# Attention phase of a three-phase kernel: the rate goes into the clip, one exponential serves two heads, and queries and keys are stacked by common instructions, with a copy on GpSimd

## The chip, the cores and the metric

The kernel runs on one core of one Trainium2 chip. A core has TensorE (matrix multiplications and transposes), VectorE, ScalarE, GpSimd and a DMA queue engine (SyncE), which run their own instruction streams and wait for one another by semaphores. The metric is the device time of one execution in microseconds, lower is better.

## The reference

A tower of four state-space layers makes `h` (2048 tokens in 8 sequences of 256, 256 features). The second phase, to which the change belongs, adds an attention whose scores are Gaussian kernels of the distance between query and key. With H = 16 heads of D = 16:

```python
qh = (q @ Wq).reshape(Bq, Sq, H, D).transpose(0, 2, 1, 3)      # likewise kh, vh
q_norm = jnp.sum(qh * qh, axis=-1, keepdims=True)              # likewise k_norm
qk = jnp.einsum('bhsd,bhtd->bhst', qh, kh)
dist = jnp.maximum(q_norm - 2.0 * qk + jnp.swapaxes(k_norm, -2, -1), 0.0)
scores = jnp.exp(-gamma[None, :, None, None] * SCALE * dist)
scores = jnp.where(mask, scores, 0.0)                          # mask: triu, k=1
out = jnp.einsum('bhst,bhtd->bhsd', scores, vh)
return out.transpose(0, 2, 1, 3).reshape(Bq, Sq, H * D) @ Wo
```

The input `q` is the layer norm of `h`. A third phase, two layers of windowed attention with a gated feed-forward part, follows.

## The kernel before, in words

`attention_phase` handles the 8 sequences (s = 0 to 7) one after the other, each as two tiles (t = 0, 1) of 128 tokens, in a software pipeline. Every engine has a function `half(h)` that lists, in a fixed order written by hand, what it does for the sequences that are in flight; TensorE's half h projects sequence h, turns sequence h - 1 and scores sequence h - 2. TensorE runs halves 2 to 10 in the block after the tower (the first sequence's part runs earlier, from `opening` in the tower's last steps and from `first`). GpSimd's and VectorE's half with number h + 3, and ScalarE's with number h + 4, hold the work that belongs to TensorE's half h. Below, "half 2" and so on are TensorE's numbers.

All matmuls are done in split precision: a value is rounded to float32r (the "hi" part) and the remainder ("lo") is kept beside it. For the distances the split is folded into the contraction: each head has a row of ROW = 64 columns per token in `qs` and `ks`. In `qs` it holds q hi, q hi again, q lo, the squared norm's hi and lo, two ones and zeros; in `ks` it holds -2k hi, -2k lo, -2k hi again, two ones, the norm's hi and lo and zeros. One matmul over these 64 rows then gives q_norm - 2 qk + k_norm. The steps for one tile:

- `project_qk` (TensorE) writes queries and keys, 512 columns, into one PSUM bank.
- `square` (ScalarE) and `norms` (VectorE) make the 32 squared norms.
- `query_hi` and `key_hi` (ScalarE, lines 1138, 1139, 1146, 1147) write the hi parts, each twice: four copies of 256 columns.
- `stack` (VectorE, lines 1309 to 1320) writes the lo parts and the norms: six instructions.
- `turn` (TensorE, line 925) transposes eight pairs of heads, queries or keys of one tile, into two banks. `turned_q` and `turned_k` (1024 columns each) copy the result to `qt` and `kt`. ScalarE does `turned_q` for both tiles and `turned_k` for tile 1, VectorE `turned_k` for tile 0 (line 1328).

Per sequence the heads go in eight pairs c: `distances(s, c, b)` (lines 938, 941) fills two banks with 384 columns per head, `clip` (VectorE, line 1336, 768 columns) takes the maximum with 0 into `dist`, `kernel_exp` (ScalarE, line 1178) makes one exponential of 384 columns per head with the scale operand `gsc[:, h:h + 1]`, `mask` (GpSimd, line 1476) clears the masked triangles, and `values(s, q, b)` (lines 957, 959) multiplies four heads by the values; the result goes through `output_hi`, `output_lo`, `project_out` and `add_output` into X. A clip needs the exponentials of two pairs earlier, since `dist` holds two pairs.

TensorE's order in half h, with b = h - 1 and c = h - 2, is: `project_v` of both tiles, `turn_x`, `distances(c, 2)`, `turn(b, 0, 0)`, `distances(c, 3)`, `turn(b, 0, 1)`, `turn(b, 1, 0)`, `distances(c, 4)`, `turn(b, 1, 1)`, `distances(c, 5)`, `values(c, 0)`, `distances(c, 6)`, `values(c, 1)`, `distances(c, 7)`, `project_out`, `distances(b, 0)`, `values(c, 2)`, `project_qk` of tile 0, `distances(b, 1)`, `values(c, 3)`, `project_qk` of tile 1. In `turn(b, t, i, bank)` i = 0 are the queries and i = 1 the keys. `values(c, 0)` writes the bank that `turn(b, 1, 0)` used and so waits for `qt_done`, `turned_q(b, 1)`.

GpSimd also does `scale_h` and `bias_h` (the tower's last norm, 512 columns each), `rstd`, and in its half h + 3 the order is: `bias_h`, `qkv_rest` (in four of the halves, a split of the third phase's weights), masks 2, 3 and 4, `scale_h`, masks 5 and 6, `rstd`, mask 7, mask 0 of the next sequence, `rstd`, mask 1. `scale_h` is there up to half 5 and `bias_h` up to half 6. Right after its first such list, between mask 1 and the `bias_h` that belongs to half 2, stands `masks()`, which fills constants of the third phase.

## Time and profile before

| | |
|---|---|
| median of 3 runs | 1275.93 us (1275.78 to 1276.22) |
| profiled execution, own time | 1278.31 us |
| its span, first to last instruction | 1276.4 us |
| mean granted TensorE clock | 0.983 of full speed |
| busy: TensorE / VectorE / ScalarE / GpSimd | 1209.8 / 984.7 / 860.2 / 621.2 us |
| turnings of the second phase | from 511.8 to 644.5 us of the span |
| exponentials of the second phase | from 526.6 to 661.7 us of the span |

The profile is of one execution. "Busy" of an engine is time in which one of its instructions ran, matmuls with their modelled ends. A time in brackets after an instruction is the idle time of its engine before it, with the instruction that ended it.

### The profile page before, as it was taken

The numbers are of one execution on the slowest core, as the hardware profiler recorded it, in microseconds if no ns is written. First come the engines' busy times: TensorE is split into PE (matmuls) and PEld (weight loads), VectorE is DVE, ScalarE is ACT, GpSimd is POOL, SyncE is SP. The second block draws the span as 40 slices with busy tenths as digits, with TensorE's granted clock in tenths as the row PEclk, the third lists the DMA queues.
The fourth block names the chain that finished last, engine by engine and source line by source line (L and its number), as shares of the span: only waits on it lengthen the run. The fifth ranks groups of instructions, "written<-read, shape, count | busy, mean of one in ns | idle before, by whom it ended". The sixth has DMA issues, their size and how long they took to land.

```text
span 1276.4 us, 26138 instructions
## 1 busy us (share of the span) xinstructions
PE 1209.8 (95%) x8899; PEld 1028.5 (81%) x8899; DVE 984.7 (77%) x2624; ACT 860.2 (67%) x1989; POOL 621.2 (49%) x678
## 2 busy tenths in 40 slices
PE   5999999999999999799978799999999999999998
PEld 3799988988888989577756567888888888888898
DVE  5767676666667777789878988888888888888754
ACT  2455766675556556689964668778777777777764
POOL 6523441361145243455434568556655567556543
PEclk9899999999999999899989999999999999999999
DMA  7400010001000000300110002000100000000001
GB/s 172 115 2 15 2 66 0 14 33 33 0 8 1 1 1 1 77 10 18 58 54 17 1 5 95 6 5 6 48 3 6 22 6 13 22 17 18 22 10 42
DMA packets 39615, 33.25 MB, mean 26 GB/s; under 512 B 16774, under 2 KB 36178, under 8 KB 39506
## 3 DMA queue, kind: packets, MB, share of 16 engines
q1 hardware_dynamic: 38610, 29.74, 7.7%
q0 software_dynamic: 768, 2.10, 1.0%
q8 instruction: 60, 0.98, 0.3%
q14 instruction: 49, 0.40, 0.1%
q10 hardware_dynamic: 128, 0.04, 0.0%
HBM read 25.84 MB, written 4.19 MB: 24 GB/s over the span
## 4 chain that ended last, share of the span: by engine, by line
PE 45%; DVE 6%; issue 3%; POOL 2%; ACT 2%; DVEq 0%; ACTq 0%; POOLq 0%
PE w_ps_p L1914 3%; PE w_ring L1975 3%; PE w_ring L1976 3%; PE w_ring L1873 3%; PE w_ring L1977 3%; PE w_ring L1875 3%; PE w_ring L1874 3%; PE w_ps_a L1932 2%; PE w_ring L1987 2%; PE a_ps L925 2%; PE w_ps_d L1907 2%; PE w_ps_d L1904 2%; PE w_ring L1891 2%; PE w_ring L1988 2%; PE w_ring L1991 1%
## 5 line engine op out<-in xcount | busy, mean ns | idle before, releaser
L392 ACT ACTIVATE t_gf<-t_ps_f,t_fb_cur 128x512 f32<-128x512 f32 x128 | 87.9, 687 | 159.8 <-PE t_ps_f L298 156.6
L542 DVE TENSOR_TENSOR t_g_lo<-t_gf,t_g_hi 128x512 fp32r<-128x512 f32 x128 | 93.3, 730 | 69.3 <-ACT t_g_hi L394 68.9
L311 PE MATMUL t_ps_o<-t_w_hi,t_g_hi 128*128 128x256 f32 x512 | 144.6, 282 | 0.1
L312 PE MATMUL t_ps_o<-t_w_lo,t_g_hi 128*128 128x256 f32 x512 | 143.0, 279 | 0.0
L313 PE MATMUL t_ps_o<-t_w_hi,t_g_lo 128*128 128x256 f32 x512 | 142.9, 279 | 0.0
L695 POOL TENSOR_TENSOR t_rs<-t_ve,t_neghalf 128x4 f32<-128x4 f32 x32 | 40.9, 1277 | 159.8 <-DVE t_ve L503 158.2
L296 PE MATMUL t_ps_f<-t_nh,t_w_hi 128*128 128x512 f32 x256 | 102.6, 401 | 1.5 <-DVE t_nl L518 0.8
L2988 POOL TENSOR_TENSOR w_m<-w_m 128x512 f32<-128x512 f32 x64 | 84.2, 1316 | 36.9 <-DVE w_m L2631 36.8
L298 PE MATMUL t_ps_f<-t_nl,t_w_hi 128*128 128x512 f32 x256 | 100.3, 392 | 0.0
L297 PE MATMUL t_ps_f<-t_nh,t_w_lo 128*128 128x512 f32 x256 | 100.0, 391 | 0.0
L311 PEld LDWEIGHTS t_ps_o<-t_w_hi,t_g_hi 128*128 128x128 f32 x512 | 96.2, 188 | 4.1 <-issue 0.9
L312 PEld LDWEIGHTS t_ps_o<-t_w_lo,t_g_hi 128*128 128x128 f32 x512 | 96.7, 189 | 2.5
L313 PEld LDWEIGHTS t_ps_o<-t_w_hi,t_g_lo 128*128 128x128 f32 x512 | 96.8, 189 | 0.0
L2674 DVE COPY w_pt<-w_ps_p 128x384 f32<-128x384 f32 x128 | 70.5, 551 | 31.4 <-PE w_ps_p L1914 29.9
L1975 PE MATMUL w_ring<-w_nh,w_w_hi 128*128 128x256 f32 x318 | 93.5, 294 | 0.0
L1976 PE MATMUL w_ring<-w_nh,w_w_lo 128*128 128x256 f32 x318 | 88.8, 279 | 0.0
L1977 PE MATMUL w_ring<-w_nl,w_w_hi 128*128 128x256 f32 x318 | 88.7, 279 | 0.0
L2999 POOL TENSOR_TENSOR w_pr<-w_pr,w_rinv 128x256 f32<-128x256 f32 x64 | 39.3, 614 | 101.0 <-DVE w_rinv L2668 101.0
L1873 PE MATMUL w_ring<-qkv_hi,w_ah 128*128 128x512 f32 x188 | 80.6, 429 | 6.7 <-DVE w_al L2613 5.7
L3004 POOL TENSOR_TENSOR w_h_lo<-w_gate,w_h_hi 128x256 fp32r<-128x256 f32 x75 | 54.6, 737 | 60.1 <-ACT w_h_hi L2413 60.1
L394 ACT ACTIVATE t_g_hi<-t_gf 128x512 fp32r<-128x512 f32 x128 | 80.9, 632 | 4.1
L1178 ACT ACTIVATE a_e<-a_dist,a_gsc 128x384 f32<-128x384 f32 x128 | 70.2, 621 | 8.3 <-DVE a_dist L1336 6.8
(369 smaller groups left out, 4285.0 us busy)
## 6 DMA issues: line engine op xcount, KB each, us to landing
t_raw<-in_L_tok_w SPq DMA_DIRECT2D x8, 1024.0 KB, 5.4
out<-X SPq DMA_DIRECT2D x14, 256.0 KB, 2.2
raw<-in_L_ffn_wqkv SPq DMA_DIRECT2D x2, 1536.0 KB, 6.9
raw<-in_L_ffn_w SPq DMA_DIRECT2D x4, 640.0 KB, 4.8
w_raw_o<-out SPq DMA_DIRECT2D x8, 256.0 KB, 2.8
w_xs<-X SPq DMA_DIRECT2D x14, 127.0 KB
w_raw<-in_L_ffn_w SPq DMA_DIRECT2D x2, 640.0 KB
t_raw_d<-in_L_tok_D SPq DMA_DIRECT2D x4, 256.0 KB
```

Source lines behind the costliest of these rows:

```text
L296: pe.matmul(ps_f[:, j % 2, :], w1_hi[:, c, col], nh[1][:, c, :], start=(c == 0), stop=False)
L297: pe.matmul(ps_f[:, j % 2, :], w1_lo[:, c, col], nh[1][:, c, :], start=False, stop=False)
L298: mm = pe.matmul(ps_f[:, j % 2, :], w1_hi[:, c, col], nl[1][:, c, :], start=False, stop=(c == DC - 1))
L311: pe.matmul(out, g_hi[:, j % 4, tok], w2_hi[:, j, :], start=(j == 0 and t % 2 == 0), stop=False, skip_group_check=True)
L312: pe.matmul(out, g_hi[:, j % 4, tok], w2_lo[:, j, :], start=False, stop=False, skip_group_check=True)
L313: mm = pe.matmul(out, g_lo[:, j % 4, tok], w2_hi[:, j, :], start=False, stop=(j == FC - 1 and t % 2 == 1), skip_group_check=True)
L392: act.activation(gf[:, j % 2, :], ps_f[:, j % 2, :], ACT.Gelu, bias=fb_cur[:, j:j + 1]).then_inc(pf_free, 1)
L542: dve.tensor_tensor(g_lo[:, j % 4, :], gf[:, j % 2, :], g_hi[:, j % 4, :].bitcast(F32), ALU.subtract).then_inc(g_split, 1)
L1873: pe.matmul(ring[:, RB[b], :], ah[:, c, tok], qkv_hi[:, c, cols], start=(c == 0), stop=False)
L1975: pe.matmul(dst, w1_hi[:, c, u, cols], n_hi[:, c, :], start=(j % 2 == 0 and c == 0), stop=False, skip_group_check=True)
L1976: pe.matmul(dst, w1_lo[:, c, u, cols], n_hi[:, c, :], start=False, stop=False, skip_group_check=True)
L1977: mm = pe.matmul(dst, w1_hi[:, c, u, cols], n_lo[:, c, :], start=False, stop=(j == chunks[-1] and c == DC - 1), skip_group_check=True)
```

## The change: one exponential per pair, common stacking, a copy on GpSimd

The rows for queries and keys now lie in one tensor `qk[t]`, at a distance of KEYS = 17 * 64 columns, so that one access pattern (`pair`) reaches the same or different columns of both. Keys are no longer multiplied by -2; instead the constant columns hold -0.5, so that the matmul gives -1/2 of the distance. The clip takes the minimum with 0 and multiplies by 2 * gamma * SCALE in the same instruction, and the exponential of both heads of a pair is one instruction of 768 columns without a scale operand. `query_hi` and `key_hi` become one `stack_hi` of 512 columns; the second copy of the hi parts (the twin) is made by GpSimd's `stack_twin`, for sequence 0 by ScalarE. TensorE's `turn` waits for `twin` as well. VectorE's `stack` has three instructions instead of six. `turned_k` of tile 0 moves from VectorE to ScalarE, between exponentials 2 and 3; for sequence 0 it stays where it was.

```diff
-        qs = [sb(f"qs{t}", [P, H, ROW], F32R) for t in range(ST)]
-        ks = [sb(f"ks{t}", [P, H, ROW], F32R) for t in range(ST)]
+        KEYS = (H + 1) * ROW
+        qk = [sb(f"qk{t}", [P, 2 * KEYS + ROW], F32R) for t in range(ST)]
...
+        def pair(t, q_at, k_at, n):
+
+            apart = KEYS + k_at - q_at
+            both = qk[t][:, q_at:q_at + 2 * apart].rearrange("p (i w) -> p i w", i=2)
+            return both[:, :, 0:H * ROW].rearrange("p i (h r) -> p i h r", r=ROW)[:, :, :, 0:n]
...
             def turn(s, t, i, b):
                 pe.wait_ge(stacked, 2 * s + t + 1)
-                src = ks[t] if i else qs[t]
+                pe.wait_ge(twin, 2 * s + t + 1)
+                src = stacked_rows(t, i)
...
-            def query_hi(s, t, b):
+            def stack_hi(s, t, b):
                 act.wait_ge(qk_full, 2 * s + t + 1)
                 if s:
                     act.wait_ge(qs_full, 2 * s + t - 1)
-                q = ps[:, 2 * b, 0:D].rearrange("p (h d) -> p h d", h=H)
-                act.activation(qs[t][:, :, 0:HD], q, ACT.Copy)
-                act.activation(qs[t][:, :, HD:2 * HD], q, ACT.Copy).then_inc(q_hi, 1)
-
-            def key_hi(s, t, b):
-                act.wait_ge(qk_full, 2 * s + t + 1)
-                if s:
                     act.wait_ge(ks_full, 2 * s + t - 1)
-                k = ps[:, 2 * b, D:2 * D].rearrange("p (h d) -> p h d", h=H)
-                act.activation(ks[t][:, :, 0:HD], k, ACT.Copy, scale=-2.0)
-                act.activation(ks[t][:, :, 2 * HD:3 * HD], k, ACT.Copy, scale=-2.0).then_inc(k_hi, 1)
+                both = ps[:, 2 * b, :].rearrange("p (i h d) -> p i h d", i=2, d=HD)
+                if s == 0:
+                    act.activation(pair(t, HD, 2 * HD, HD), both, ACT.Copy).then_inc(twin, 1)
+                act.activation(pair(t, 0, 0, HD), both, ACT.Copy).then_inc(qk_hi, 1)
...
-                for x in range(2):
-                    h = 2 * c + x
-                    ins = act.activation(e[:, h % SLOTS, :], dist[:, h % BANKS, :], ACT.Exp, scale=gsc[:, h:h + 1])
-                ins.then_inc(exp_done, 1)
+                h = 2 * c
+                act.activation(e[:, h % SLOTS:h % SLOTS + 2, :], dist[:, h % BANKS:h % BANKS + 2, :], ACT.Exp).then_inc(exp_done, 1)
...
                 if real(f):
-                    query_hi(f, 0, 0)
-                    key_hi(f, 1, 1)
+                    stack_hi(f, 1, 1)
                     square(f, 1, 1)
                     keep_values(f, 0, 3)
-                    query_hi(f, 1, 1)
                     keep_values(f, 1, 2)
...
                 if real(g):
                     kernel_exp(g, 2)
+                if real(f):
+                    turned_k(f, 0, 0)
+                if real(g):
                     kernel_exp(g, 3)
...
                     square(e, 0, 0)
-                    key_hi(e, 0, 0)
+                    stack_hi(e, 0, 0)
...
             def stack(s, t, b):
...
+                dve.tensor_tensor(pair(t, 2 * HD, HD, HD), ps[:, 2 * b, :].rearrange("p (i h d) -> p i h d", i=2, d=HD),
+                                  pair(t, 0, 0, HD).bitcast(F32), ALU.subtract).then_inc(qk_read, 1)
+                both = nrm[t][:, :].rearrange("p (i h d) -> p i h d", i=2, d=1)
+                hi, lo = pair(t, 3 * HD, 3 * HD + 2, 1), pair(t, 3 * HD + 1, 3 * HD + 3, 1)
+                dve.wait_ge(nrm_done, n + 1)
+                dve.tensor_copy(hi, both).then_inc(nrm_hi, 1)
                 dve.wait_ge(nrm_hi, n + 1)
+                dve.tensor_tensor(lo, both, hi.bitcast(F32), ALU.subtract).then_inc(stacked, 1)
...
-                dve.tensor_scalar(dist[:, two, :], ps[:, 2 * b:2 * b + 2, 0:SCORES], 0.0, None, ALU.max).then_inc(relu_done, 1)
+                rate = gsc[:, 2 * c:2 * c + 2].unsqueeze(2).broadcast_to([P, 2, SCORES])
+                dve.scalar_tensor_tensor(dist[:, two, :], ps[:, 2 * b:2 * b + 2, 0:SCORES], 0.0, rate, ALU.min, ALU.mult).then_inc(relu_done, 1)
...
-                dve.tensor_scalar(gsc[:, :], gam[:, :], -SCALE, None, ALU.mult).then_inc(s_gsc, 1)
+                dve.tensor_scalar(gsc[:, :], gam[:, :], 2.0 * SCALE, None, ALU.mult).then_inc(s_gsc, 1)
+                dve.wait_ge(s_gsc, 1)
...
-                if real(d):
-                    turned_k(d, 0, 0)
                 if real(e):
                     clip(e, 4, 3)
...
+            def stack_twin(s, t):
+                pool.wait_ge(qk_hi, 2 * s + t + 1)
+                pool.tensor_copy(pair(t, HD, 2 * HD, HD), pair(t, 0, 0, HD).bitcast(F32)).then_inc(twin, 1)
...
                 if real(c):
                     bias_h(c)
+                if e > 0 and real(e):
+                    stack_twin(e, 1)
                 if 0 <= g < PARTS // 2:
                     qkv_rest(2 * g)
...
                 if real(e):
                     mask(e, 0)
+                if d > 0 and real(d):
+                    stack_twin(d, 0)
                 if real(a):
                     rstd(a, 0)
```

In `pads` the constant columns are set by three memsets per tile instead of four, to -0.5 where they were 1.0. `opening` and `first` call `stack_hi` where they called `key_hi` and `query_hi`.

## Rows read from the trace of the kernel before

**Rows 1.** The page, its first line.
```profile
span 1276.4 us, 26138 instructions
```
**Rows 2.** Stretches: busy time, instructions, granted clock, DMA share; half 5 to 6.
```profile
588.76:606.41 17.65, 17.09 (x168) 12.97 (x168) 16.73 (x36) 16.70 (x37) 10.16 (x15) 1.00 0.05 16
```
**Rows 3.** Chain of waits, 586.3 to 606.4 us: start, us, what.
```profile
593.95 0.61 ACT a_e L1178
...
595.26 1.27 POOL X L1464
```
**Rows 4.** Timeline of TensorE: start, us, instruction, count, idle before.
```profile
589.69 1.04 PE L925 MATMUL a_ps<-a_ident,a_qs 128*128 128x128 f32 x8
...
592.45 0.64 PE L959 MATMUL a_ps<-a_e,a_v 128*32 128x256 f32 x8
...
597.18 0.64 PE L959 MATMUL a_ps<-a_e,a_v 128*32 128x256 f32 x8 [0.38 <-POOL a_e L1476]
...
604.92 1.09 PE L925 MATMUL a_ps<-a_ident,a_qs 128*128 128x128 f32 x8
...
639.74 1.09 PE L925 MATMUL a_ps<-a_ident,a_qs 128*128 128x128 f32 x8 [0.56 <-ACT a_v L1153]
```
**Rows 5.** Timeline of ScalarE, 588 to 607 us.
```profile
588.39 1.07 ACT L1160 ACTIVATE a_qt<-a_ps 128x1024 fp32r<-128x1024 f32 x1
589.31 2.17 ACT L1178 ACTIVATE a_e<-a_dist,a_gsc 128x384 f32<-128x384 f32 x4
591.34 1.05 ACT L1160 ACTIVATE a_qt<-a_ps 128x1024 fp32r<-128x1024 f32 x1
...
604.55 1.17 ACT L1178 ACTIVATE a_e<-a_dist,a_gsc 128x384 f32<-128x384 f32 x2
```
**Rows 6.** Groups by form: busy us, mean ns | idle before.
```profile
L1178 ACT ACTIVATE a_e<-a_dist,a_gsc 128x384 f32<-128x384 f32 x128 | 70.2, 621 | 8.3 <-DVE a_dist L1336 6.8 <-PE a_ps L957 0.4
L445 ACT ACTIVATE wa_whi<-raw 128x768 fp32r<-128x768 f32 x2 | 1.7, 853 | 0.0
L1138 ACT ACTIVATE a_qs<-a_ps 128x256 fp32r<-128x256 f32 x16 | 6.4, 401 | 0.0
L1131 ACT ACTIVATE a_sq<-a_ps 128x512 f32<-128x512 f32 x16 | 9.6, 598 | 1.7 <-PE a_ps L901 1.6
L1336 DVE TENSOR_SCALAR a_dist<-a_ps 128x768 f32<-128x768 f32 x64 | 60.3, 952 | 8.6 <-PE a_ps L941 5.0 <-ACT a_e L1178 2.7 <-issue 0.2
L1316 DVE SCALAR_TENSOR_TENSOR a_ks<-a_ps,a_ks 128x256 fp32r<-128x256 f32 x16 | 6.6, 413 | 0.0
L1293 DVE TENSOR_TENSOR a_nl<-a_ps,a_nh 128x512 fp32r<-128x512 f32 x8 | 5.4, 679 | 0.0
L1328 DVE CAST a_kt<-a_ps 128x1024 fp32r<-128x1024 f32 x8 | 9.7, 1215 | 5.8 <-PE a_ps L925 5.8
L173 POOL CAST t_d_hi<-t_raw_d 128x512 fp32r<-128x512 f32 x3 | 1.8, 612 | 0.0
```
**Rows 7.** Timeline of GpSimd, around 606 us.
```profile
605.79 0.64 POOL L1476 TENSOR_SCALAR_AFFINE_SELECT a_e<-a_e 128x512 f32<-128x512 f32 x1 [4.58 <-ACT a_e L1178]
606.40 1.28 POOL L1469 TENSOR_TENSOR X<-X,a_fb 128x512 f32<-128x512 f32 x1
```
**Rows 8.** Half 2 and its end: TensorE and GpSimd in time, and a stretch.
```profile
534.05 1.04 PE L925 MATMUL a_ps<-a_ident,a_qs 128*128 128x128 f32 x8
...
534.62 1.28 POOL L1469 TENSOR_TENSOR X<-X,a_fb 128x512 f32<-128x512 f32 x1
...
540.58 0.38 PE L938 MATMUL a_ps<-a_qt,a_kt 64*128 64x256 f32 x2 [1.36 <-DVE a_dist L1336]
...
542.00:543.00 1.00, 1.00 (x17) 0.39 (x9) 0.93 (x5) 1.00 (x4) 1.00 (x2) 0.50 0.00 0
...
554.36 1.04 PE L925 MATMUL a_ps<-a_ident,a_qs 128*128 128x128 f32 x8
```
**Rows 9.** Timeline of VectorE: the last clip.
```profile
660.15 0.96 DVE L1336 TENSOR_SCALAR a_dist<-a_ps 128x768 f32<-128x768 f32 x1 [0.40 <-ACT a_e L1178]
```

More of the change, by code:

```diff
@@ L850, in attention_phase @@
         t_full, nh_done, n_split = sem("t_full"), sem("nh_done"), sem("n_split")
-        qk_full, v_full, sq_done, q_hi, k_hi, qk_read, v_done = (sem(x) for x in ("qk_full", "v_full", "sq_done", "q_hi", "k_hi", "qk_read", "v_done"))
+        qk_full, v_full, sq_done, qk_hi, twin, qk_read, v_done = (sem(x) for x in ("qk_full", "v_full", "sq_done", "qk_hi", "twin", "qk_read", "v_done"))
         nrm_done, nrm_hi, stacked, qs_full, ks_full, qt_done = (sem(x) for x in ("nrm", "nrm_hi", "stacked", "qs_full", "ks_full", "qt_done"))
@@ L870, in real, with stacked_rows @@
             return 0 <= s < M
+        def stacked_rows(t, i):
+            return qk[t][:, i * KEYS:i * KEYS + H * ROW].rearrange("p (h r) -> p h r", r=ROW)
+        def pair(t, q_at, k_at, n):
+            apart = KEYS + k_at - q_at
+            both = qk[t][:, q_at:q_at + 2 * apart].rearrange("p (i w) -> p i w", i=2)
+            return both[:, :, 0:H * ROW].rearrange("p i (h r) -> p i h r", r=ROW)[:, :, :, 0:n]
         def opening_loads(sp):
@@ L1243, in opening @@
                     square(0, 0, 0)
-                    key_hi(0, 0, 0)
+                    stack_hi(0, 0, 0)
                 if j == 5:
-                    query_hi(0, 0, 0)
                     square(0, 1, 1)
                 if j == 6:
-                    key_hi(0, 1, 1)
-                    query_hi(0, 1, 1)
+                    stack_hi(0, 1, 1)
                 if j == 7:
@@ L1262, in first @@
                 square(1, 0, 0)
-                key_hi(1, 0, 0)
+                stack_hi(1, 0, 0)
             return half, opening, first
@@ L1303, in stack @@
                 n = 2 * s + t
[L1304 to L1306 removed]
+                dve.wait_ge(qk_hi, n + 1)
                 if s:
                     dve.wait_ge(qs_full, n - 1)
[L1309 to L1310 removed]
                     dve.wait_ge(ks_full, n - 1)
[L1312 to L1316 removed]
+                dve.tensor_tensor(pair(t, 2 * HD, HD, HD), ps[:, 2 * b, :].rearrange("p (i h d) -> p i h d", i=2, d=HD),
[4 more added lines that the diff above has]
+                dve.tensor_copy(hi, both).then_inc(nrm_hi, 1)
                 dve.wait_ge(nrm_hi, n + 1)
[L1318 to L1321 removed]
+                dve.tensor_tensor(lo, both, hi.bitcast(F32), ALU.subtract).then_inc(stacked, 1)
             def turned_k(s, t, b):
@@ L1351, in pads @@
                 for t in range(ST):
-                    dve.memset(qs[t][:, :, 3 * HD + 2:3 * HD + 4].bitcast(F32), 1.0)
-                    dve.memset(qs[t][:, :, 3 * HD + 4:ROW].bitcast(F32), 0.0)
-                    dve.memset(ks[t][:, :, 3 * HD:3 * HD + 2].bitcast(F32), 1.0)
-                    ins = dve.memset(ks[t][:, :, 3 * HD + 4:ROW].bitcast(F32), 0.0)
+                    dve.memset(stacked_rows(t, 0)[:, :, 3 * HD + 2:3 * HD + 4].bitcast(F32), -0.5)
+                    dve.memset(stacked_rows(t, 1)[:, :, 3 * HD:3 * HD + 2].bitcast(F32), -0.5)
+                    ins = dve.memset(pair(t, 3 * HD + 4, 3 * HD + 4, ROW - 3 * HD - 4).bitcast(F32), 0.0)
                 ins.then_inc(s_pad, 1)
```

16 lines of the change are left out of this document (removed).

## The prediction, made before the changed kernel was run

> **What bounds the kernel now.** The page comes first: span 1276.4 us [rows 1]. The change touches only the second phase, which opens inside the tower's last steps and has its last clip at 660 us [rows 9], so the next view is the stretches, cut from one turning of tile 0's keys to the next. One such stretch, a "half", takes 17.65 us, with TensorE busy 17.09, VectorE 16.73, ScalarE 16.70, GpSimd 10.16 [rows 2]. Three engines are nearly full, so totals don't decide: the waits of TensorE do. The chain of waits through this half shows one place where TensorE's end is not set by TensorE: the second exponential of pair 4, its mask, `scale_h` and the next mask, and then the `values(c, 2)` matmuls, which start 0.38 us after TensorE was ready [rows 3, 4]. The other such place is before the next half's turnings, where a tile's kept values are late: 0.56 us in the last half that has any [rows 4].
>
> I count time t from the start of `turn(b, 0, 0)`, which is 604.92 us for one half [rows 4] and, a length of 17.65 us earlier [rows 2], 587.27 us for the half that I follow. In it `turn(b, 1, 0)` starts at t = 2.42, `values(c, 0)` at 5.18, `values(c, 2)` at 9.91 [rows 4]. On ScalarE `turned_q(b, 0)` starts at 1.12, exponentials 2 and 3 at 2.04, `turned_q(b, 1)` at 4.07; it ends at 5.12, so `values(c, 0)`, which overwrites its bank, follows at once [rows 4, 5].
>
> **The clip.** It becomes a scalar_tensor_tensor of 768 columns, PSUM and a broadcast SBUF operand. Before: 952 ns a clip. The same kind of instruction with 256 columns takes 413 ns, and the PSUM-SBUF subtraction of 512 takes 679: 266 ns for 256 columns, so 768 should cost 945 [rows 6]. I take no change. The other end, half rate, is a rival below. The reduced `pads`, and `scale_gamma`'s wait, lie within the tower's last steps under TensorE's matmuls; I take zero. If uncovered they are a few short memsets, under 1 us once.
>
> **The exponentials.** Two of 384 columns with a scale operand take 621 ns each. A group of four spans 2.17 us, so each costs (2.17 - 0.62)/3 = 0.52 us of the queue and 0.10 overlaps the next [rows 5, 6]. One of 768 without that operand is nearest to the 768-column copy, 853 ns [rows 6]: 0.75 of the queue. A pair goes from 1.03 to 0.75 in the queue, 0.28 less, 2.2 us over eight pairs. The ends: 0.69 of the queue (three quarters of the 1024-column copy's 0.92, below [rows 5]) and 1.04 (nothing saved against two). [...]
>
> **The stacking.** Per tile four 256-column copies go (401 ns each, 0.30 of the queue with the same overlap) and one 512-column one comes, like the 598 ns square of 512 from PSUM [rows 6], 0.50 of the queue: 0.7 us less per tile, 1.4 per half. VectorE's six instructions become three: 679 instead of twice 0.41, and two small ones, in all within 0.1 us of before. The new last one waits for the one before it with nothing between; I take zero and allow 0.2 more. `turned_k(b, 0)` leaves VectorE (1.215 us [rows 6]) for ScalarE, where a 1024-column copy takes 0.92 of the queue (588.39 to 589.31 [rows 5]). So VectorE falls from 16.7 to about 15.5 us per half and ScalarE by 2.2 + 1.4 - 0.9 = 2.7 us. Neither pays by itself; what counts is the order.
>
> **The queue of ScalarE.** From 1.12: `turned_q(b, 0)` to 2.04, exponential 2 to 2.79, the new `turned_k(b, 0)` to 3.71, exponential 3 to 4.46, `turned_q(b, 1)` to 5.51 and a semaphore (0.06): `values(c, 0)` at 5.57 instead of 5.18, **+0.39 us**. The moved copy sits in front of the copy that frees the bank; TensorE waits. With 0.69 for an exponential this is +0.3, with 1.04 it is +1.0.
> From there the mask chain: exponential 4 started 0.98 after `values(c, 0)` (593.43 against 592.45) and its pair ended at 594.56 [rows 3, 5], 2.11 after it; new 0.98 + 0.85 = 1.83. The rest (mask, `scale_h`, mask, start) stays at 2.62 (594.56 to 597.18 [rows 3, 4]). So `values(c, 2)` starts at 5.57 + 1.83 + 2.62 = 10.02 against 9.91: **+0.11** per half, and -0.05 from the one copy ahead of the kept values: +0.06. Halves 2 to 5 have `scale_h`; 6 and 7 have not, and there the +0.39 goes through whole. Halves 3, 4, 5: +0.2; 6 and 7: +0.8. At the start of half 8 the wait on kept values of 0.56 [rows 4] loses the two query copies that stood before it: -0.4, and VectorE's earlier clip of pair 2 gives -0.2.
>
> **The twin on GpSimd.** Nearest row: GpSimd's 512-column cast, 612 ns [rows 6]; a tensor_tensor of 512 takes 1.28 [rows 7]: these are the ends. I take 0.61, it being the same operation, with doubt about its runs of 16 columns. `stack_twin(e, 1)` stands behind the mask of pair 1 and `bias_h`; behind it wait masks 2 and 3, and TensorE's `turn(b, 1, 0)`. Exponential 1 started at 604.55, t = -0.37 [rows 5]; without the two query copies ahead it starts at about -0.9 and ends at -0.05. Mask to 0.65, `bias_h` (1.28 [rows 7]) to 1.93, twin to 2.54, turning at 2.6 instead of 2.42; `values(c, 0)` by TensorE's own work then at 2.6 + 2.76 = 5.4, under ScalarE's 5.57. In steady halves the twin is hidden up to 0.82 us. Twin 0 stands where GpSimd was idle for 4.58 us [rows 7]: nothing.
> In half 2 it is not hidden. `masks()` of the window phase and `bias_h` come between mask 1 and the twin: `bias_h` starts at 534.62, `turn(1, 1, 0)` at 534.05 [rows 8]. New: `bias_h` 0.75 earlier, 533.87, its end 535.14, the twin's 535.75, the turning 535.8: +1.75, and 0.28 back over exponential 4: **+1.45 us**.
>
> **The end.** From 645 us on the chain runs through clips and exponentials. The last clip starts 0.40 us after VectorE was free, for an exponential [rows 9]. Three such steps (mask 7 of half 8, pairs 2 to 4, pairs 5 to 7) are each about 0.28 shorter: **-0.85 us**.
>
> **Sum**: 1.45 + 0.2 + 0.8 - 0.4 - 0.2 - 0.85 = +1.0 us on the span, 1277.4. The profiled execution's own time was 1278.31, 1.9 above its span and 2.4 above the median of the runs, so the median becomes 1275.93 + 1.0 = **1276.9 us**.
>
> **Rivals.** What a measurement tells from no change here is about 0.2%, 2.55 us.
> (a) The twin is slow. With D us instead of 0.61, half 2 gives D - 0.61 more and five halves D - 0.82 each. At the tensor_tensor's 1.28: 0.67 + 2.3 = 3.0, median 1279.9. It decides from D = 1.04 on. For it: 16-column runs, no row shows them on GpSimd; against it: the cast row.
> [...]
> (c) The other side: the stretch at half clock at 541 us does not occur, -2.7, and `values(c, 0)` is not delayed (ScalarE's queue runs 0.39 us ahead of the sum above, in each of halves 3 to 7, -1.9): 1.0 - 2.7 - 1.9 = -3.6, median 1272.3. It decides only if both happen, or the delay of half 2 fails to appear as well.
> (d) The clip runs at half rate: 768 columns at twice 1.04 ns, 0.8 us more each, 6.4 us per half. VectorE then needs 22 us per half instead of 15.5 and bounds it: +4.3 us in seven halves and a tail, +30, median 1306. Against it: the 413 and 679 ns rows, both with PSUM and SBUF inputs. [...]
>
> **How the numbers follow.** The sum as told, or near it: 0.50. (a) or (b), or both: 0.32. (c): 0.14. (d): 0.04. The predicted time is the first case's, 1276.9 (its own range 1275 to 1278.4). The range for 8 in 10 reaches up to (a), with (b) in part, and down by most of one clock stretch: 1273.6 to 1280.6. Faster takes (c), 0.14; slower takes (a), (b), (d), 0.36 less a little that stays under the bound: 0.34; same 0.52.
>
> **What would show it.** `values(c, 0)` must start some 5.5 us after `turn(b, 0, 0)`, released by ScalarE's query copy; the turning of tile 1's queries in half 2 must wait about 1.7 us for GpSimd; the twin at 0.6 us; exponentials of 0.85; clips of 0.95; halves 3 to 5 within 0.2 us of 17.65. The prediction is wrong if the turnings wait in every half, if the granted clock falls at other places, or if halves come out shorter than 17.5.

## The result: slower by 0.4%, just outside the range, and the profile after

The changed kernel took 1280.66 us (median of 11 runs, 1277.14 to 1282.31), the kernel before in the same session 1275.57 (11 runs, 1272.16 to 1278.97). The ratio is 1.004, 95% interval 1.0026 to 1.0053. The forecast was 1276.9 and no clear change; its range ended at 1280.6.

The profiled execution took 1279.54 us with a span of 1277.5, only 1.1 more than the span before [rows 1]. That pair misleads: the one profiled before (1278.31) lay 2.7 us above its median of that session, this one 1.1 below. An execution's span follows its mean granted clock (of the kernel before, over all sessions, 34 executions at 0.983 had a mean span of 1276.9 and 30 at 0.989 one of 1271.6), so I compare spans at one clock. At 0.986, 18 executions of the kernel before had a mean span of 1274.7, and 4 of the changed kernel 1278.3: **+3.6 us** for the change itself. Over the five clocks that both kernels have (23 executions of the changed one) the mean difference is +3.6 too; at single clocks it lies between 2.6 and 4.6.

The page of the kernel after, its first line and the row of engines:

```profile
span 1277.5 us, 25980 instructions
...
PE 1207.7 (95%) x8899; PEld 1026.3 (80%) x8899; DVE 978.3 (77%) x2567; ACT 843.7 (66%) x1886; POOL 631.1 (49%) x692
```

Groups of instructions by form, after; they answer to [rows 6]:

```profile
L1331 DVE SCALAR_TENSOR_TENSOR a_dist<-a_ps,a_gsc 128x768 f32<-128x768 f32 x64 | 60.0, 951 | 17.5 <-PE a_ps L952 15.9 <-ACT a_e L1180 1.0
...
L1180 ACT ACTIVATE a_e<-a_dist 128x768 f32<-128x768 f32 x64 | 53.2, 840 | 15.9 <-DVE a_dist L1331 14.4 <-PE a_ps L968 0.9
...
L1152 ACT ACTIVATE a_qk<-a_ps 128x512 fp32r<-128x512 f32 x16 | 9.5, 596 | 7.1 <-PE a_ps L911 7.1
...
L1474 POOL CAST a_qk<-a_qk 128x512 fp32r<-128x512 f32 x14 | 8.6, 611 | 4.7 <-ACT a_qk L1152 4.7
...
L1281 DVE TENSOR_SCALAR a_ve<-a_mv 128x2 f32<-128x2 f32 x16 | 6.0, 372 | 0.6
```

Every duration came as forecast: clip 951 ns (952 before), exponential 840 (0.85 forecast), joined copy 596, twin 611. The last row is the odd one. `ve`, the little instruction that adds epsilon to a variance (128 x 2), has a mean of 372 ns, and takes 0.17 us when alone. I had not looked at it.

Stretches of the kernel after, each from one `turn(b, 0, 0)` to the next, halves 3, 4 and 5 (length; busy time of TensorE, its weight loads, VectorE, ScalarE and GpSimd; granted clock, DMA share, GB/s; such a half took 17.65 in [rows 2]):

```profile
551.01:569.47 18.46, 17.34 (x172) 13.09 (x168) 16.73 (x35) 14.47 (x24) 12.12 (x16) 1.00 0.05 15
569.47:587.34 17.87, 17.19 (x173) 13.00 (x169) 16.45 (x36) 14.89 (x25) 12.08 (x16) 1.00 0.05 17
587.34:605.72 18.38, 17.21 (x173) 12.99 (x169) 16.49 (x31) 14.44 (x25) 11.37 (x15) 1.00 0.05 16
```

ScalarE has 2 us less to do per half, TensorE's work is the same, and the halves are longer: TensorE waits more. Where, the timeline of TensorE after shows:

```profile
530.31 1.09 PE L936 MATMUL a_ps<-a_ident,a_qk 128*128 128x128 f32 x8
...
534.64 1.06 PE L936 MATMUL a_ps<-a_ident,a_qk 128*128 128x128 f32 x8 [1.84 <-POOL a_qk L1474]
...
551.01 1.09 PE L936 MATMUL a_ps<-a_ident,a_qk 128*128 128x128 f32 x8
...
553.86 1.06 PE L936 MATMUL a_ps<-a_ident,a_qk 128*128 128x128 f32 x8 [0.35 <-POOL a_qk L1474]
...
556.62 0.64 PE L970 MATMUL a_ps<-a_e,a_v 128*32 128x256 f32 x8
...
561.35 0.38 PE L949 MATMUL a_ps<-a_qt,a_kt 64*128 64x256 f32 x2 [0.72 <-DVE a_dist L1331]
...
561.73 0.64 PE L970 MATMUL a_ps<-a_e,a_v 128*32 128x256 f32 x8
...
571.42 2.02 PE L936 MATMUL a_ps<-a_ident,a_qk 128*128 128x128 f32 x16 [0.47 <-DVE a_dist L1331]
```

In half 3 `turn(b, 1, 0)` waits 0.35 us for the twin, `values(c, 0)` starts at t = 5.61 (t counts from the half's `turn(b, 0, 0)`), and the distances before `values(c, 2)` wait 0.72 us for a clip, so that `values(c, 2)` starts at t = 10.72 where 10.02 was forecast. Half 5 repeats this (0.35 and 0.73). Why the clip is late, the timelines of VectorE and of GpSimd in the same half say:

```profile
555.34 0.96 DVE L1331 SCALAR_TENSOR_TENSOR a_dist<-a_ps,a_gsc 128x768 f32<-128x768 f32 x1 [1.26 <-PE a_ps L952]
...
558.86 0.25 DVE L1278 BATCH_NORM_AGGREGATE a_mv<-a_st 128x2 f32<-128x6 f32 x2
559.14 1.30 DVE L1281 TENSOR_SCALAR a_ve<-a_mv 128x2 f32<-128x2 f32 x1
560.36 1.81 DVE L1331 SCALAR_TENSOR_TENSOR a_dist<-a_ps,a_gsc 128x768 f32<-128x768 f32 x2
```
```profile
553.10 0.61 POOL L1474 CAST a_qk<-a_qk 128x512 fp32r<-128x512 f32 x1
...
559.13 1.28 POOL L1457 TENSOR_TENSOR X<-a_xn,a_fs 128x512 f32<-128x512 f32 x1
560.37 0.64 POOL L1469 TENSOR_SCALAR_AFFINE_SELECT a_e<-a_e 128x512 f32<-128x512 f32 x1
```

`ve` starts at 559.14, 0.01 us after GpSimd's `scale_h` (559.13), and ends with it (560.44 against 560.41): 1.30 us for an instruction of 0.17. Clip 6 stands behind it, and TensorE's distances wait for that clip. The mask of pair 5, for which `values(c, 2)` waited in the kernel before, was done at 561.01, t = 10.00, before TensorE came. The same happens at 595.47 in half 5. In half 4 `ve` takes 0.17, and that half is the shortest of the three. It is still 0.22 us longer than before, and there another small VectorE instruction, the last of `stack`, started 0.05 us after a mask and ended 0.07 us after it, 0.66 us for 0.22; the clip behind it is the one for which TensorE waits 0.47 at 571.42. VectorE and GpSimd:

```profile
569.84 0.66 DVE L1315 TENSOR_TENSOR a_qk<-a_nrm,a_qk 128x32 fp32r<-128x32 f32 x1
```
```profile
569.79 0.64 POOL L1469 TENSOR_SCALAR_AFFINE_SELECT a_e<-a_e 128x512 f32<-128x512 f32 x1 [2.42 <-ACT a_e L1180]
```

In the kernel before the same two instructions stand like this, VectorE and then GpSimd:

```profile
577.52 0.17 DVE L1281 TENSOR_SCALAR a_ve<-a_mv 128x2 f32<-128x2 f32 x1
577.61 1.82 DVE L1336 TENSOR_SCALAR a_dist<-a_ps 128x768 f32<-128x768 f32 x2
```
```profile
577.63 1.30 POOL L1464 TENSOR_TENSOR X<-a_xn,a_fs 128x512 f32<-128x512 f32 x1
```

There `ve` was 0.11 us ahead of `scale_h`, and nothing was blocked: `ve` took 0.17 us, `scale_h` 1.30, and the two clips beside `scale_h`, which read PSUM, were not longer either (0.96 and 0.95 us, the mean of all being 0.952 [rows 6]). The kernel before escaped by 0.05, 0.11 and 0.06 us in its halves 3, 4 and 5. In the changed kernel's half 3 `ve` and `scale_h` agree in time, 1.30 us beside 1.28. The rows show that `ve` was held until GpSimd's instruction ended. By what it was held no row shows.

Halves 2 to 7 in the profiles, in us: before 20.32, 17.66, 17.65, 17.66, 17.18, 17.64; after 20.70, 18.46, 17.87, 18.38, 17.55, 17.22.

### The profile page after: what moved, and what is told of

It is laid out like the page before. It is cut to its first block, busy times and chain, and to the rows that moved or that the text cites. A ratio compares the mean times of both kernels' runs of the same rounds, so it can differ in the third digit from the quotient of the medians.

```text
span 1277.5 us, 25980 instructions
## 1 busy us (share of the span) xinstructions
PE 1207.7 (95%) x8899; PEld 1026.3 (80%) x8899; DVE 978.3 (77%) x2567; ACT 843.7 (66%) x1886; POOL 631.1 (49%) x692
## 4 chain that ended last, share of the span: by engine, by line
PE 45%; DVE 6%; issue 3%; POOL 3%; ACT 2%; DVEq 0%; ACTq 0%; POOLq 0%
PE w_ps_p L1915 3%; PE w_ring L1874 3%; PE w_ring L1976 3%; PE w_ring L1876 3%; PE w_ring L1977 3%; PE w_ring L1978 3%; PE w_ring L1875 3%; PE w_ps_a L1933 2%; PE w_ring L1988 2%; PE w_ps_d L1908 2%; PE w_ps_d L1905 2%; PE w_ring L1892 2%; PE w_ring L1989 2%; PE w_ring L1992 1%; PE w_ring L1944 1%
## 5 line engine op out<-in xcount | busy, mean ns | idle before, releaser
L1876 PE MATMUL w_ring<-qkv_hi,w_al 128*128 128x512 f32 x188 | 75.6, 402 | 0.0
```

Source lines behind the costliest of these rows:

```text
L1876: mm = pe.matmul(ring[:, RB[b], :], al[:, c, tok], qkv_hi[:, c, cols], start=False, stop=(c == DC - 1))
```

## The experiments

The theory after the first profiles: the twin's wait makes TensorE's distances and so VectorE's clip 4 later, `ve` falls behind `scale_h`, is blocked, and clip 6 with the distances behind it is late. Rivals: the moved `turned_k`, the place of clip 6, the joined exponentials, or only the clock. In the table "halves 3 to 7" is their sum in the profile, and the ratio is to the kernel before on the same chip. Half 2 can be compared only between runs with the same clock in it: those of same_again, before_look, keys_back, clip_first and two_exps, and of the first profiles of both kernels, hold a stretch at the lower clock (granted 0.50), the others none (1.00 throughout).

| run | median us | ratio, 95% interval | half 2 | halves 3 to 7 |
|---|---|---|---|---|
| same_again (the kernel before) | 1276.24 | 0.9996, 0.9981 to 1.001 | 19.07 | 87.76 |
| after_again (the changed kernel) | 1280.09 | 1.0025, 1.0011 to 1.0039 | 19.16 | 89.52 |
| keys_back | 1280.52 | 1.0028, 1.0016 to 1.004 | 20.66 | 90.01 |
| clip_first | 1280.68 | 1.003, 1.0018 to 1.0041 | 20.66 | 90.55 |
| twin_early | 1274.81 | 0.9985, 0.9972 to 0.9999 | 17.70 | 87.63 |
| scale_late | 1275.97 | 0.9996, 0.9982 to 1.001 | 18.69 | 87.42 |
| exp_only | 1276.58 | 1.0007, 0.9991 to 1.0024 | 17.27 | 89.23 |
| early_keys | 1274.01 | 0.9983, 0.9968 to 0.9998 | 17.53 | 87.24 |
| early_scale | 1273.88 | 0.9989, 0.9976 to 1.0002 | 17.25 | 87.50 |
| early_keys_scale | 1272.92 | 0.9979, 0.9965 to 0.9993 | 17.12 | 86.28 |
| stack_only | 1279.92 | 1.0034, 1.0019 to 1.0048 | 18.06 | 90.14 |
| stack_order | 1274.43 | 0.9986, 0.9972 to 1.0001 | 17.55 | 88.01 |
| two_exps | 1282.11 | 1.0037, 1.0022 to 1.0051 | 21.23 | 90.54 |
| before_scale_late | 1274.62 | 0.9991, 0.9975 to 1.0007 | 17.59 | 87.75 |
| before_look (one execution) | 1277.12 | | 19.10 | 87.79 |

**The two kernels again.** Expected of the kernel before:

> The kernel before, unchanged. In the two profiles the changed kernel is only 1.1 us longer, while the timed runs say about 5. Theory: the stretches at the lower granted clock differ from execution to execution, and the profile of before had more of them (mean granted clock 0.983 against 0.987). Expected: the spans of this kernel's executions rise as their mean granted clock falls, by 0.5 to 1 us for each 0.001, and at 0.987 it takes about 1274 us of span against 1277.5 to 1278.7 for the changed one. Rival: the profile pair is right and the timed difference is drift; then executions of before at 0.987 lie at 1276 to 1277. Ratio to before within 0.2% of 1 for both.

Expected of the changed kernel on a second chip:

> The changed kernel, unchanged. Theory L (lock): in halves 3 and 5 the last small instruction of VectorE's norm statistics starts as GpSimd's scale_h does and ends with it (1.3 us instead of 0.17), as in the first profile; halves 3 to 5 take 18.46, 17.87 and 18.38 us within 0.1. In half 2 the turning waits 1.8 us for the twin and the stretch at the lower clock follows: 20.7 us. Ratio to before 1.003 to 1.004. Rival: the lengths of the halves differ from execution to execution by more than 0.3 us, then the single profiles prove little.

At a granted clock of 0.987, 24 executions of the kernel before had a mean span of 1273.8, as expected, and 7 of the changed one 1277.5. Halves 3 to 7 repeat to 0.05 us in each kernel (87.79, 87.76, 87.79 in three profiles before; 89.48, 89.52 in two after), so the pattern of meetings belongs to the program and not to the execution: `ve` took 1.31 and 1.32 us at 558.68 and 595.03 again. Half 2 is another matter. Its length depends on whether TensorE's clock falls in it: the changed kernel's took 20.70 us with a stretch at 0.50 (after) and 19.16 at 1.00 throughout (after_again). Two windows of 7 us show both cases, first the kernel before (same_again), then the changed one (after_again); the last three columns are granted clock (1.00 is full speed), DMA share and GB/s:

```profile
540.00:547.00 7.00, 6.12 (x49) 3.90 (x50) 5.99 (x14) 5.89 (x14) 4.57 (x7) 0.76 0.00 0
```
```profile
540.00:547.00 7.00, 5.41 (x68) 3.42 (x61) 6.86 (x18) 5.90 (x11) 5.38 (x8) 1.00 0.01 4
```

One more profile of the kernel before was taken for this:

> The kernel before, one more profile. Theory: the clock's low stretch at 540 to 547 us in half 2, seen in two profiles of this kernel, isn't bound to it: if it is missing here, half 2 takes 17.3 to 17.7 us; if it is there, 19 to 20.5. Halves 3 to 7 sum to 87.8 within 0.1 either way.

Its half 2 took 19.10 us with the low stretch, the third of three profiles of that kernel that have it. I have no profile of it without. The nearest is before_scale_late, below, whose other halves are as before: 17.59 at a granted clock of 1.00.

**Moving the twin.** twin_early issues the twin copy of tile 1 before the mask of pair 1:

```diff
-                if e > 0 and real(e):
-                    stack_twin(e, 1)
...
+                if d > 0 and real(d):
+                    stack_twin(d, 1)
                 if real(e):
                     mask(e, 1)
```

> The changed kernel, with stack_twin of tile 1 ahead of the mask of pair 1 instead of behind it and bias_h. Theory: the waits of the turnings for GpSimd (1.84 us in half 2, 0.35 in half 3, about 0.4 in half 6) vanish; half 2's wait passes into the end nearly whole, the others are hidden by ScalarE's queue: -1.5 to -2 us against the changed kernel, ratio to before about 1.0025. Rival: the wait of half 2 was hidden by the low clock stretch that followed it; then no change, 1.004.

0.9985, where 1.0025 was expected: the whole loss was gone, and 1.9 us more, because the meetings, which the expectation left out, went with the waits. TensorE waits for no twin, `values(c, 2)` starts at t = 9.95, and in the timeline of VectorE `ve` is held for 0.49 us, by a mask and no longer by `scale_h`:

```profile
557.16 0.49 DVE L1281 TENSOR_SCALAR a_ve<-a_mv 128x2 f32<-128x2 f32 x1
557.56 1.81 DVE L1331 SCALAR_TENSOR_TENSOR a_dist<-a_ps,a_gsc 128x768 f32<-128x768 f32 x2
```

Against the changed kernel's half 3, `ve` starts 0.55 us earlier (t = 7.58 for 8.13) and `scale_h` only 0.10 earlier (8.02 for 8.12). So in the changed kernel it is the twin's wait that puts `ve` behind `scale_h`.

**Moving `scale_h`.** This leaves the twin and its waits, and takes the meeting with `scale_h` away:

```diff
+                if real(f):
+                    mask(f, 5)
                 if real(b):
                     scale_h(b)
                 if real(f):
-                    mask(f, 5)
                     mask(f, 6)
```

> The changed kernel, with GpSimd's scale_h behind the mask of pair 5 instead of ahead of it. Theory L: the small VectorE instruction now meets the mask (0.64 us) and not scale_h (1.28 us), its longest time is about 0.65 us, distances(b, 0) waits 0.1 us or less in halves 3 and 5, and the mask chain is 1.28 us shorter: halves 3 to 5 at about 17.6 us, -2 us against the changed kernel, ratio 1.002. Theory S (only ScalarE's queue counts): values(c, 0) still starts 5.6 us after the turning, and the halves gain only what the mask chain gives, 0.3 us in half 4 and none in 3 and 5. Half 2's wait of 1.8 us for the twin stays by both.

0.9996, less than the 1.002 expected, and halves 3 to 7 fell from 89.5 to 87.42. Halves 3 and 5, with the meetings, fell by 0.91 and 0.84 us, half 4 by 0.39; there the last instruction of `stack` is no longer held (all 16 of them take 0.22 us in this run). TensorE still waited 1.83 us for the twin in half 2 and 0.34 to 0.40 in three later ones. VectorE and GpSimd in half 3:

```profile
557.47 0.17 DVE L1281 TENSOR_SCALAR a_ve<-a_mv 128x2 f32<-128x2 f32 x1
```
```profile
556.85 1.38 POOL L1469 TENSOR_SCALAR_AFFINE_SELECT a_e<-a_e 128x512 f32<-128x512 f32 x2 [1.69 <-ACT a_e L1180]
558.20 1.28 POOL L1457 TENSOR_TENSOR X<-a_xn,a_fs 128x512 f32<-128x512 f32 x1
```

`scale_h` now starts 0.7 us behind `ve`. So the twin's waits of 0.35 us cost next to nothing by themselves; they are given back at the later waits of the same half. It is the meeting that costs. But the edit also lets mask 5 go earlier, which could gain on its own. The control is the same edit in the kernel before:

> The kernel before with the one edit of scale_late: scale_h issued after mask(f, 5). Theory (in the changed kernel that edit gains by taking the meeting of ve and scale_h away; here there is none but in half 2's neighbourhood): 0.999 to 1.001, halves within 0.15 of 17.66. Rival (it gains by an earlier mask(f, 5), which releases values(c, 2), for which PE waits 0.38 us in each half here): those waits gone, halves of 17.3, ratio 0.9975 to 0.9985.

0.9991 with 1 inside the interval, and halves 3 to 7 at 87.75 against 87.79. Waits for a mask moved, the sum did not. And twin_early, which leaves `scale_h` ahead of mask 5, starts `values(c, 2)` as early as scale_late does (t = 9.95 and 9.92 in half 3). The gain in the changed kernel is that of the meetings. The stretch of half 2 of before_scale_late:

```profile
530.81:548.40 17.59, 15.62 (x161) 11.54 (x157) 17.00 (x42) 16.71 (x37) 10.34 (x18) 1.00 0.02 2
```

**Both moves** (early_scale):

> The changed kernel with tile 1's twin copy issued on GpSimd before mask(e, 1) and with scale_h issued after mask(f, 5), so both the copy's wait and the meeting of VectorE's ve with GpSimd's scale_h are taken away. Theory (two costs, the copy's waits in half 2 and in halves 3 to 5, and the meetings, that share one cause): by the runs with one of the two edits (0.9985 and 0.9996 of the kernel before) the second edit has little left to take, ratio 0.997 to 0.999, no ve above 0.6 us, no twin wait above 0.1 us, halves 17.4 to 17.7. Rival (the two costs add): 0.9955 to 0.997. Rival (the timed difference lies elsewhere): at or above 1.000.

0.9989, with halves 3 to 7 at 87.50: either edit alone takes the meetings' 2 us, and the second adds nothing there. They do not add: in halves 3 to 5 the twin's wait costs by the meetings that it brings about. Only in half 2 is the twin's wait a cost of its own: 18.69 with `scale_h` late, 17.25 with both.

**Undoing other parts.** keys_back gives `turned_k` of tile 0 back to VectorE, first ScalarE's half, then VectorE's:

```diff
                     kernel_exp(g, 2)
-                if real(f):
-                    turned_k(f, 0, 0)
-                if real(g):
                     kernel_exp(g, 3)
...
+                if real(d):
+                    turned_k(d, 0, 0)
```

> The changed kernel, but turned_k of tile 0 stays on VectorE. Theory S (ScalarE's queue holds up values(c, 0), as the prediction had it): values(c, 0) starts 5.2 us after turn(b, 0, 0) instead of 5.6 to 5.8, halves 3 to 7 are 0.3 to 0.4 us shorter each, ratio to before about 0.0015 lower than the changed kernel's, 1.0025. Theory V (VectorE's clip of pair 6 is late, because the small instruction before it waits for GpSimd's scale_h): VectorE has 1.2 us more work and the mask chain still runs earlier than in the kernel before, so the collision stays or becomes more frequent, distances(b, 0) waits 0.5 us or more, and the ratio stays at 1.004 or is higher.

1.0028, as slow as the change. `ve` was blocked in halves 3, 4 and 5 (1.30, 1.32, 1.29 us), and each time the distances waited 0.72 to 0.78. `values(c, 0)` did not come earlier: t = 5.61 in half 3, as in the changed kernel, so ScalarE's queue had not held it there. The moved copy is not the cause. clip_first issues clip 6 before the statistics of tile 1, so that it stands ahead of `ve`:

```diff
+                if real(f):
+                    clip(f, 6, 3)
...
-                    clip(f, 6, 3)
```

> The changed kernel, with VectorE's clip of pair 6 moved ahead of norm_stats(c, 1). Theory V: distances(b, 0) no longer waits for the clip in halves 3 and 5 (0.72 us in half 3), those halves fall to about 17.9 us, -1.2 to -1.6 us in all, ratio to before 1.003. Theory S: the halves are set by ScalarE's queue and the mask chain, no change, 1.004.

1.003 was expected and came, the shorter halves did not: 18.68, 18.83 and 17.98 us. The wait of the distances before `values(c, 2)` was gone in half 3 (t = 10.08), and the next distances waited 0.81 instead. `scale_h` is over before `ve` starts, but now two masks hold `ve`, 0.56 and 0.65 us, each with a later clip behind it:

```profile
561.81 0.56 DVE L1281 TENSOR_SCALAR a_ve<-a_mv 128x2 f32<-128x2 f32 x1
...
564.21 0.65 DVE L1281 TENSOR_SCALAR a_ve<-a_mv 128x2 f32<-128x2 f32 x1
```

exp_only is the kernel before with the rate in the clip and one exponential per pair, and nothing else:

```diff
-                for x in range(2):
-                    h = 2 * c + x
-                    ins = act.activation(e[:, h % SLOTS, :], dist[:, h % BANKS, :], ACT.Exp, scale=gsc[:, h:h + 1])
-                ins.then_inc(exp_done, 1)
+                h = 2 * c
+                act.activation(e[:, h % SLOTS:h % SLOTS + 2, :], dist[:, h % BANKS:h % BANKS + 2, :], ACT.Exp).then_inc(exp_done, 1)
...
-                dve.tensor_scalar(dist[:, two, :], ps[:, 2 * b:2 * b + 2, 0:SCORES], 0.0, None, ALU.max).then_inc(relu_done, 1)
+                rate = gsc[:, 2 * c:2 * c + 2].unsqueeze(2).broadcast_to([P, 2, SCORES])
+                dve.scalar_tensor_tensor(dist[:, two, :], ps[:, 2 * b:2 * b + 2, 0:SCORES], 0.0, rate, ALU.max, ALU.mult).then_inc(relu_done, 1)
...
```

> The kernel before with one part of the change: the rate in the clip (maximum, times the negative rate) and one exponential per pair. Theory L: clips cost the same (0.95 us), exponentials 0.84 instead of two of 0.62; values(c, 0) stays at 5.2 us after the turning; the mask chain is 0.28 us shorter, but scale_h then starts 0.28 us earlier, before the small VectorE instruction, which it blocks for about 1 us: halves 3 to 5 become 0.3 to 0.6 us longer. With 0.85 us from the end the ratio is 0.9995 to 1.001. Rival: no blocking, each half 0.28 us shorter and the end 0.85: -2.3 us, 0.998.

1.0007, no change, though ScalarE has 2 us less per half. The timelines of VectorE and GpSimd in half 3 say where it went:

```profile
555.95 1.04 DVE L1277 TENSOR_SCALAR a_ve<-a_mv 128x2 f32<-128x2 f32 x1
```
```profile
555.68 1.29 POOL L1462 TENSOR_TENSOR X<-a_xn,a_fs 128x512 f32<-128x512 f32 x1
```

Here there is no twin, and the meeting comes from the other side: a shorter exponential releases the mask and then `scale_h` sooner, and `scale_h` overtakes `ve`, in halves 3, 4 and 5 (18.09, 18.24, 18.16 us). Half 2 (17.27, against 17.59 at the same clock in before_scale_late) and the stretch from the start of half 8 to the window phase (22.57 for 23.53) are shorter, by 1.3 us together, and halves 3 to 7 are 1.4 longer: the one pays for the other. So my theory was too narrow. The margin of 0.05 to 0.11 us is lost by an earlier `scale_h` as well as by a later `ve`. two_exps is the opposite, the changed kernel with the two exponentials and a plain clip:

```diff
...
-                h = 2 * c
-                act.activation(e[:, h % SLOTS:h % SLOTS + 2, :], dist[:, h % BANKS:h % BANKS + 2, :], ACT.Exp).then_inc(exp_done, 1)
+                for x in range(2):
+                    h = 2 * c + x
+                    ins = act.activation(e[:, h % SLOTS, :], dist[:, h % BANKS, :], ACT.Exp, scale=gsc[:, h:h + 1])
+                ins.then_inc(exp_done, 1)
...
-                rate = gsc[:, 2 * c:2 * c + 2].unsqueeze(2).broadcast_to([P, 2, SCORES])
-                dve.scalar_tensor_tensor(dist[:, two, :], ps[:, 2 * b:2 * b + 2, 0:SCORES], 0.0, rate, ALU.min, ALU.mult).then_inc(relu_done, 1)
+                dve.tensor_scalar(dist[:, two, :], ps[:, 2 * b:2 * b + 2, 0:SCORES], 0.0, None, ALU.min).then_inc(relu_done, 1)
...
```

> The changed kernel with the exponentials as before (two per pair, 0.55 each, the rate as their scale) and a clip by tensor_scalar; the joined stack, the twin on GpSimd and the moved turned_k stay. Theory (the loss comes from the twin's waits and the meetings they cause; joined exponentials give ScalarE some 0.26 us per pair back): slower than or as slow as the change, 1.002 to 1.005. Rival (the longer clips, 0.95 for 0.93 us, and the single exponential, which frees its second head later, cost the time): back to 0.999 to 1.001.

1.0037: no blocked `ve` above 0.57 us, but the twin, released later, now holds TensorE in earnest, 2.08 us in half 2 and 0.55 to 0.60 in halves 3 to 6, of which the first three take 18.40 us each. In half 4:

```profile
573.48 0.30 PE L936 MATMUL a_ps<-a_ident,a_qk 128*128 128x128 f32 x1 [0.55 <-POOL a_qk L1476]
```

The ratios of the two kernels overlap, but at one clock they part: at 0.985, three executions of two_exps had a mean span of 1281.1 and five of the changed kernel 1279.0. The joined exponentials are thus a gain in the changed kernel, not a part of its loss.

**No copy on GpSimd.** In stack_only the twin is a second ScalarE copy of 512 columns inside `stack_hi`:

```diff
-                if s == 0:
-                    act.activation(pair(t, HD, 2 * HD, HD), both, ACT.Copy).then_inc(twin, 1)
+                act.activation(pair(t, HD, 2 * HD, HD), both, ACT.Copy).then_inc(twin, 1)
                 act.activation(pair(t, 0, 0, HD), both, ACT.Copy).then_inc(qk_hi, 1)
...
```

> The changed kernel with the twin copy as a second ScalarE activation in stack_hi in every half, and none on GpSimd: what is left of the change is the joined copy, the rate in the clip, the single exponential and the moved turned_k. Theory (the twin copy on GpSimd costs its wait in half 2, about 1.7 us, and shifts ve onto scale_h in later halves): no wait for the twin, half 2 at 17.3 to 18.0, and a ratio of 0.999 to 1.001. ve and scale_h can still meet, as they did in the run with the exponentials alone, since both hang on the same phase. Rival (the moved turned_k and the longer ScalarE queue cost the time): 1.002 to 1.005 with values(c, 0) more than 6 us after the turning's start.

My expectation failed: 1.0034, with halves 2 to 4 of 18.1 us each. The rival's number came but not its sign, since `values(c, 0)` started at t = 5.5. ScalarE and then TensorE at the end of half 4:

```profile
584.11 0.60 ACT L1150 ACTIVATE a_qk<-a_ps 128x512 fp32r<-128x512 f32 x1 [0.78 <-PE a_ps L911]
584.60 0.59 ACT L1151 ACTIVATE a_qk<-a_ps 128x512 fp32r<-128x512 f32 x1
585.08 0.60 ACT L1142 ACTIVATE a_sq<-a_ps 128x512 f32<-128x512 f32 x1
585.56 0.68 ACT L1157 ACTIVATE a_v<-a_ps 128x256 f32<-128x256 f32 x2
```
```profile
586.01 0.66 PE L903 MATMUL a_ps<-a_ident,a_xn 128*128 128x128 f32 x4 [0.53 <-ACT a_v L1157]
```

Both copies and the square run between the projection and the first `keep_values`, for which TensorE waits in every half (0.53 us here, 0.53 to 0.58 in all six). stack_order issues the second copy of tile 1 behind `keep_values(f, 0, 3)` and that of tile 0 behind `stack_hi`, and VectorE's `stack`, whose `qk_read` lets TensorE write the bank again, waits for both. The edit for tile 1, against the changed kernel:

```diff
                     stack_hi(f, 1, 1)
                     square(f, 1, 1)
                     keep_values(f, 0, 3)
+                    copy_twin(f, 1, 1)
                     keep_values(f, 1, 2)
```

> The changed kernel without any copy on GpSimd: the twin copy is a ScalarE activation of its own, issued after keep_values(f, 0, 3) for tile 1 and after stack_hi for tile 0; VectorE's stack waits for it, as both read one bank. Theory (in stack_only the two copies ahead of square and keep_values held PE's turn_x for 0.53 us in every half, about 0.43 per half and 2.6 over six): that wait falls to under 0.1, halves of 17.4 to 17.8, ratio 0.999 to 1.001. Rival (the joined copy and the moved turned_k cost the time wherever the twin is made): halves of 18 or more and 1.002 to 1.004.

0.9986, with halves 3 to 7 at 88.01 and no wait for kept values before the start of half 8, where the kernel before has one too [rows 4]. It was a little better than expected. The same work is 0.5% apart by the places of two copies in a queue. The change without GpSimd is as good as the change with the twin early.

**The best version.** early_keys is twin_early with `turned_k` of tile 0 back on VectorE; early_keys_scale has the late `scale_h` too.

> The changed kernel with the twin of tile 1 ahead of the mask of pair 1 and with turned_k of tile 0 back on VectorE. Theory S: values(c, 0) at 5.2 us, 0.3 us less per half than with the early twin alone, ratio 0.9970. Theory L: VectorE's chain is 1.2 us longer again, its small instruction starts after scale_h and is blocked for about 1 us; halves 3 to 5 at 18 us or more, ratio 0.9995 or above.

> As early_keys (0.9983), with scale_h issued after mask(f, 5). Theory: early_keys still showed one meeting, ve of 1.32 us in half 3 with a distance wait of 0.78; without it that half falls from 17.93 to about 17.5, ratio 0.9975 to 0.9982. Rival: the ring of turns sets the pace and nothing comes, 0.9983 to 0.999.

early_keys came between its two theories (0.9983): `values(c, 0)` was earlier in half 3 (t = 5.07), and one `ve` was still blocked by `scale_h`, 1.32 us in half 3, which took 17.93 us. With `scale_h` late that half took 17.40 and the sum fell from 87.24 to 86.28, 1.5 below the kernel before. Its ratio of 0.9979 (0.9965 to 0.9993) is the lowest here. Returning `turned_k`, useless as long as the meetings were there, is worth 1.2 us of the sum once they are gone (87.50 to 86.28).

## Why the prediction was wrong

Step by step, by its own terms:

- **Durations.** Right, all four within 0.02 us. Rivals (a), slow twin, and (d), clip at half rate, are refuted by the rows above. That the time came out near (a)'s 1279.9 is a coincidence. ScalarE's busy time fell by 2.1 us per half, less than the forecast 2.7.
- **ScalarE's queue, "+0.39 us".** The number is right, the wait behind it is not: that is luck. `values(c, 0)` started at t = 5.61 in half 3 (forecast 5.57), and half 6 came out 0.37 us longer (forecast 0.39). But ScalarE's `turned_q(b, 1)` was done at t = 5.45 (forecast 5.51), first row below, and TensorE did not wait for it. TensorE itself was late: `turn(b, 1, 0)` began at t = 2.85, not 2.6, and its own work of 2.76 us ends at 5.61. The prediction had it the other way round, "5.4, under ScalarE's 5.57". keys_back, without the moved copy, has the same 5.61 in half 3 and 5.62 in half 6. Only with the twin early does ScalarE's copy hold `values(c, 0)`, at t = 5.51 in half 3, second row (twin_early).

```profile
555.43 1.03 ACT L1165 ACTIVATE a_qt<-a_ps 128x1024 fp32r<-128x1024 f32 x1
```
```profile
555.09 0.64 PE L970 MATMUL a_ps<-a_e,a_v 128*32 128x256 f32 x8 [0.37 <-ACT a_qt L1165]
```

- **Half 2.** Right: `turn(1, 1, 0)` waited 1.84 us for the twin, forecast 1.75. Without a low clock the half took 19.16 (after_again) against 17.59 (before_scale_late), +1.57 for a forecast +1.45.
- **"In steady halves the twin is hidden up to 0.82 us", and "Halves 3, 4, 5: +0.2".** This is the step that failed. The three halves took 54.71 us instead of 52.97, **+1.74**. I followed the delay to `values(c, 0)`, found that ScalarE was later anyway, and stopped. The prediction let only the mask chain decide when `values(c, 2)` starts. That chain held: mask 5 was done at t = 10.00 in half 3, where 10.02 was forecast for `values(c, 2)`. The path that it put at nothing, VectorE's queue to clip 6 and the distances that wait for it, ended last: 10.72 (10.25 and 10.73 in halves 4 and 5). The turning's 0.35 us delays the distances and clip 4 (t = 4.33, with the twin early 3.78), and VectorE's queue behind it up to `ve`. Two instructions that stood 0.05 and 0.06 us apart, `ve` on VectorE and `scale_h` on GpSimd, changed their order in halves 3 and 5, and 1.1 us of VectorE's time went with it in each (`ve` 1.30 and 1.31 us for 0.17). In half 4 it was 0.44 us at the last instruction of `stack`.
- **The kept values and the end.** Half 7 with the start of half 8 came out 0.42 shorter (forecast +0.39 and -0.4, so 0). From there to the window phase's first matmul it took 23.06 us instead of 23.53, -0.47 (forecast -0.85 and -0.2). The sign is right, together near the forecast.
- **Rival (b)**, a second or longer stretch at the lower clock in half 2: not the cause. All three profiles of the kernel before have one in half 2, of the changed kernel one of two. The sign that the prediction named for being wrong did come, though: the turning of tile 1 waited in halves 3, 5 and 6 for the twin, and in half 4 a turning waited for a clip.
- **Rival (c)**, a faster kernel, did not come. Its 2.7 us for the stretch at 541 us is half 2's 20.31 us less the 17.65 of half 5 [rows 2, 8]. That holds for that profile (17.59 at 1.00 throughout in before_scale_late), whose clock was at 0.50 for 6.8 us. With 3.4 us at 0.50 the same half took 19.07 (same_again), 1.48 more than 17.59, and the changed kernel's 20.70 against 19.16, 1.54 more.

At full clock these add up to 1.57 + 1.74 + 0.37 - 0.42 - 0.47 = +2.8 us, and at equal clock the spans differ by 3.6. Some 0.8 us is not located. From the window phase's first transposes to its first projection the profiles differ in the clock: 5.36 to 5.43 us before, granted 0.50 for the first 3 us; 4.12 and 4.47 after, granted 1.00 for the first us and mostly 0.50 from there; 3.69 at 1.00 in before_scale_late. And what follows varies by 3 us among the three profiles of the kernel before (607.7 to 610.6), which hides the 0.8. The timed medians, 5.1 and 4.0 us apart in two sessions, also hold a difference in the clocks that the executions happened to get.

What is shown: removing the meetings (scale_late, and by another way twin_early) gives all of the loss back within the interval, and the same edit does nothing where there are none. Shown in half 3 of twin_early is also that the twin's wait is what put `ve` behind `scale_h` in the changed kernel. But exp_only shows that shorter exponentials alone lose the margin too. What is not shown: by what `ve` is held.
